# A message-passing GNN on one core: how edge records are stored and fetched again

## The reference

```python
s2 = jnp.concatenate([src, dst]); d2 = jnp.concatenate([dst, src])
ef2 = jnp.concatenate([ef, ef], axis=0)
h_prev = nf
for l in range(3):
    e_in = jnp.concatenate([h_prev[s2], h_prev[d2], ef2], axis=-1)
    msg = jax.nn.leaky_relu(e_in @ We1[l]) @ We2[l]
    red = jax.ops.segment_sum(msg, d2, num_segments=N)
    n_in = jnp.concatenate([h_prev, red], axis=-1)
    out = jax.nn.leaky_relu(n_in @ Wn1[l]) @ Wn2[l]
    h_prev = out + h_prev
# result: _layernorm(x + out)
```

## Time and profile before

| | us |
|---|---|
| median of three runs | 3773.15 (3763.34 to 3774.12) |
| the profiled execution | 3767.26 |
| its span | 3765.6 |
| PE, DVE, ACT, POOL busy | 2446.1, 2741.9, 2101.1, 776.5 |
| DMA | 564.71 MB, mean 150 GB/s |

### The profile page before, as it was taken

The page is one execution under the profiler, slowest core; times in us unless marked ns, Lnnn a source line. Parts: engine busy times, 40 slices in busy tenths (PEclk is TensorE's granted clock), DMA queues, the critical chain, the costliest instruction groups (busy, mean ns, idle before and its releaser), DMA issues.

```text
span 3765.6 us, 82355 instructions
## 1 busy us (share of the span) xinstructions
PE 2446.1 (65%) x26696; PEld 2111.7 (56%) x26697; DVE 2741.9 (73%) x3306; ACT 2101.1 (56%) x4171; POOL 776.5 (21%) x826
## 2 busy tenths in 40 slices
PE   4000000000004499999999699999999799999995
PEld 4000000000004387878787488888888588888884
DVE  8965655655622499999999677777777677777775
ACT  4000000000002377877787588888888688888884
POOL 0577777777771000000000000000000000000000
PEclk9555555555555699999999899999999899999998
DMA  8111111111004277777777355555555255555553
GB/s 245 56 31 43 44 31 43 43 31 43 17 13 133 84 251 250 255 253 250 249 258 251 122 172 186 190 188 192 187 186 173 94 190 191 186 187 189 189 191 111
DMA packets 237764, 564.71 MB, mean 150 GB/s; under 512 B 52668, under 2 KB 134530, under 8 KB 237598
## 3 DMA queue, kind: packets, MB, share of 16 engines
q1 hardware_dynamic: 210174, 548.80, 43.0%
q0 software_dynamic: 27552, 15.37, 2.1%
HBM read 413.59 MB, written 150.66 MB: 150 GB/s over the span
## 4 chain that ended last, share of the span: by engine, by line
PE 47%; DVE 11%; issue 6%; SPq 3%; DMA 2%; ACT 1%; POOL 0%; DVEq 0%; ACTq 0%; POOLq 0%
PE gath L1336 17%; PE sums L1397 13%; PE sums L1336 9%; PE gath L1329 4%; DVE loop_buf L1131 3%; DVE big L1060 3%; PE sums L1329 2%; DVE loop_buf L1148 2%; SPq L539 2%; DVE gsel L1064 2%; DMA loop_buf<-ssel_d 1%; DMA nums_d<-numb 1%; PE sums L1290 1%; PE sums L1505 1%; PE sums L1506 0%
## 5 line engine op out<-in xcount | busy, mean ns | idle before, releaser
L1060 DVE SCALAR_TENSOR_TENSOR big<-big 128x768 f32<-128x768 f32 (+1 forms) x957 | 908.4, 949 | 426.8 <-ACT big L786 387.6
L1336 PE MATMUL gath<-table,gsel 128*128 x7488 | 1075.7, 273 | 0.0
L1131 DVE TENSOR_TENSOR loop_buf<-big,loop_buf 128x768 f16<-128x768 f32 x936 | 890.4, 951 | 0.0
L650 POOL DMA_INDIRECT records<-rec,rowi x784 | 750.8, 958 | 285.6 <-issue 248.3
L1397 PE MATMUL sums<-loop_buf 128*128 128x128 f16 x11232 | 782.2, 219 | 23.8 <-issue 18.1
L1336 PEld LDWEIGHTS gath<-table,gsel 128*128 128x128 f16 x7488 | 734.1, 98 | 84.9
L790 ACT ACTIVATE loop_buf<-big 128x768 f16<-128x768 f32 x936 | 781.4, 835 | 0.0
L1397 PEld LDWEIGHTS sums<-loop_buf 128*128 128x128 f16 x11232 | 650.1, 98 | 124.5 <-ACT sums L784 58.0
L786 ACT ACTIVATE big<-gath 128x512 f32<-128x512 f32 x936 | 559.1, 597 | 278.1 <-PE gath L1336 278.1
L1252 PE MATMUL sums<-table,fchunk 128*128 128x200 f16 x196 | 37.1, 366 | 877.1 <-DVE found L976 864.7
L1336 PE MATMUL sums<-table,gsel 128*128 x3744 | 564.1, 273 | 13.2 <-DVE gsel L1064 13.2
(11 more groups left out here) (174 smaller groups left out, 1657.6 us busy)
## 6 DMA issues: line engine op xcount, KB each, us to landing
gsel<-gsel_d SPq DMA_DIRECT2D x208, 576.0 KB, 3.8
loop_buf<-ssel_d SPq DMA_DIRECT2D x208, 576.0 KB, 4.7
numb<-nums_d SPq DMA_DIRECT2D x106, 576.0 KB, 4.6
gsel_d<-gsel SPq DMA_DIRECT2D x104, 576.0 KB, 5.5
ssel_d<-loop_buf SPq DMA_DIRECT2D x104, 576.0 KB, 6.5
fchunk<-feat_d SPq DMA_DIRECT2D x1260, 40.0 KB, 1.8
loop_buf<-rows_d SPq DMA_DIRECT2D x28, 896.0 KB
records<-rec,rowi POOLq DMA_INDIRECT x784
```

What stands on the lines that cost most here:

```text
L650: pool.indirect_dma_start(out=records[:, :], out_offset=bass.IndirectOffsetOnAxis(ap=rowi[:, h, g:g + 1].bitcast(U32), axis=0), in_=rec[:, ...
L1060: return dve.scalar_tensor_tensor(m, m, SLOPE, m, ALU.mult, ALU.max)
L1131: dve.tensor_tensor(m_lo[:, place, :], msg[:, place, :], m_hi[:, place, :], ALU.subtract)\
L1336: return pe.matmul(uv, gsel[:, h, (2 * tc + s) * P:(2 * tc + s + 1) * P], at[n], start=False, stop=n == 3, skip_group_check=True)
```

## The change

Records: feat_d loses the two number rows per tile and becomes 64 rows (two tiles of 32). SP stores the features of a batch in two transfers of 32 rows each. The numbers of a batch are copied to `num16` on DVE (double-buffered), transposed on PE into 64 rows of their own, in the unused half of the bank of group h = 3, copied by DVE to `numT`, and stored in one transfer of 64 rows of 256 B. `numcol` is filled from num16. POOL's reload now waits for the num16 copy, PE waits for it ahead of h = 3, and SP for numT after it has issued the features.

Layers: a part's features come in two transfers of 64 rows instead of four of 32 (in all layers); in layers 1 and 2 they are issued behind gsel and ssel instead of ahead of them.

```diff
@@ -106,7 +106,7 @@
 def build(nc, x, src, dst, ef, We1, We2, Wn1, Wn2, c_iota, c_part, c_tri, c_ident, c_tiles, c_steps, c_below, out):
 
     records = nc.dram_tensor("records", [TILES * P, RW], F16)
-    feat_d = nc.dram_tensor("feat_d", [2, RW, (TILES // 2 + F_AHEAD * PART_PAIRS) * P], F16)
+    feat_d = nc.dram_tensor("feat_d", [4 * EF, (TILES // 2 + F_AHEAD * PART_PAIRS) * P], F16)
     nums_d = nc.dram_tensor("nums_d", [(TILES + PART) * 2, P], F16)
 
     gsel_d = nc.dram_tensor("gsel_d", [TURNS * PARTS + 1, P, PART * 2 * P], F16)
@@ -257,6 +257,8 @@
 
         recc = sb("recc", [P, SLOTS_IN, PREP, CHUNK, RW], F16)
         hrow = recc[:, :, :, :, :].rearrange("p k h t f -> p (k h t f)")[:, 0:2 * RUN * P].rearrange("p (h e) -> p h e", h=2)
+        num16 = sb("num16", [P, 2, 2 * BATCH], F16)
+        numT = sb("numT", [2 * BATCH, SLOTS_IN, P], F16)
         numcol = sb("numcol", [P, TILES * 2], F16)
         lo_b = numcol[:, 0:2 * COLS].bitcast(I32)
 
@@ -353,7 +355,8 @@
         rec_hi_seq = sem("rec_hi_seq")
         moved = [sem(f"moved{h}") for h in range(2)]
         recc_in = [sem(f"recc_in{k}") for k in range(SLOTS_IN)]
-        numcol_set = sem("numcol_set")
+        num16_set = sem("num16_set")
+        numT_set = sem("numT_set")
         tr_done = sem("tr_done")
         featA_set = sem("featA_set")
         featD_set = sem("featD_set")
@@ -416,7 +419,7 @@
         T_BLOCKS = 2 * NB // T_PARTS
         WIDE = [(n, min(BANK, NODES - n * BANK)) for n in range(BANKS)]
         YSTEPS = -(-NB // 4)
-        FEAT_DMAS = 4
+        FEAT_DMAS = 2
         EDGE_DMAS, NODE_DMAS = 2 + P // EF, 2
         
 
@@ -453,6 +456,10 @@
 
             n = k * PREP + h
             return bank(n) if n < BANKS else gath
+
+        def num_bank(k):
+
+            return tr_bank(k, PREP - 1)[0:2 * BATCH, BANK // 2:BANK // 2 + P // 2]
 
 
         block = ctx.enter_context(nc.Block())
@@ -533,18 +540,15 @@
                             sp.wait_ge(featA_set, batch * 2 + 2 + BANK_AHEAD)
                             sp.wait_ge(featD_set, batch * 2 + 2 + BANK_AHEAD)
                             sp.sem_inc(sp_go, 1)
-                            sp.dma_start(feat_d[:, :, ds(batch * (PAIR_COLS * P), PAIR_COLS * P)].rearrange("a f e -> (a f) e"),
-                                         recT[slot]).then_inc(rec_out[slot], 16)
                             for a in range(2):
-                                sp.dma_start(nums_d[ds(batch * (2 * BATCH), 2 * BATCH), :]
-                                             .rearrange("(q a s) e -> a s q e", a=2, s=2)[a],
-                                             recT[slot][a * RW + 2 * EF:(a + 1) * RW, :].rearrange("s (q e) -> s q e", e=P))\
-                                  .then_inc(rec_out[slot], 16)
+                                sp.dma_start(feat_d[a * 2 * EF:(a + 1) * 2 * EF, ds(batch * (PAIR_COLS * P), PAIR_COLS * P)],
+                                             recT[slot][a * RW:a * RW + 2 * EF, :]).then_inc(rec_out[slot], 16)
+                            sp.wait_ge(numT_set, batch + 1)
+                            sp.dma_start(nums_d[ds(batch * (2 * BATCH), 2 * BATCH), :], numT[:, slot, :]).then_inc(rec_out[slot], 16)
             for slot in range(SLOTS_IN):
                 sp.wait_ge(rec_out[slot], (live_p + (1 - slot // 2)) // 2 * (16 * OUT_DMAS) + 16 * OUT_DMAS)
 
-            sp.dma_start(feat_d[:, :, ds(live_n * (ITER_PAIRS * P), F_AHEAD * PART_PAIRS * P)].rearrange("a f e -> (a f) e"),
-                         feat_d[:, :, 0:F_AHEAD * PART_PAIRS * P].rearrange("a f e -> (a f) e")).then_inc(wrap_out, 16)
+            sp.dma_start(feat_d[:, ds(live_n * (ITER_PAIRS * P), F_AHEAD * PART_PAIRS * P)], feat_d[:, 0:F_AHEAD * PART_PAIRS * P]).then_inc(wrap_out, 16)
             sp.dma_start(nums_d[ds(live_n * (ITER * 2), 2 * PART * 2), :], nums_d[0:2 * PART * 2, :]).then_inc(wrap_out, 16)
             sp.wait_ge(wrap_out, 32)
 
@@ -556,11 +560,8 @@
 
                 pair = (turn_n + p // PARTS) * ITER_PAIRS + p % PARTS * PART // 2
                 for r in range(2):
-                    for a in range(2):
-                        at = (2 * r + a) * 2 * EF
-                        sp.dma_start(fchunk[at:at + 2 * EF, p % PARTS, :],
-                                     feat_d[a:a + 1, 0:2 * EF, ds(pair * P, PART_PAIRS * P)].rearrange("a f e -> (a f) e"))\
-                          .then_inc(fchunk_in[p % PARTS], DMA)
+                    sp.dma_start(fchunk[r * 4 * EF:(r + 1) * 4 * EF, p % PARTS, :], feat_d[:, ds(pair * P, PART_PAIRS * P)])\
+                      .then_inc(fchunk_in[p % PARTS], DMA)
 
             load_numbers(0, 0)
             load_numbers(1, 1)
@@ -589,11 +590,11 @@
                                 h, part_n = p % 2, it * PARTS + p
 
                                 sp.wait_ge(sum_done, (l * live_n + it) * STEPS + p * PART_STEPS + AHEAD)
-                                load_features(it, p + F_AHEAD)
                                 sp.dma_start(gsel[:, 1 - h, :], gsel_d[ds(part_n + 1, 1), :, :].rearrange("a p e -> (a p) e"))\
                                   .then_inc(gsel_set[1 - h], DMA)
                                 sp.dma_start(ssel_part(h), ssel_d[ds(part_n, 1), :, :].rearrange("a p e -> (a p) e"))\
                                   .then_inc(ssel_set[h], DMA)
+                                load_features(it, p + F_AHEAD)
 
                 with sp.If(l < 1):
                     for h in range(2):
@@ -663,7 +664,7 @@
                             batch = it * SLOTS_IN + k
 
                             pool.wait_ge(tr_done, (batch + 1 - SLOTS_IN) * PREP + TR_AHEAD)
-                            pool.wait_ge(numcol_set, batch + 1)
+                            pool.wait_ge(num16_set, batch + 1)
                             pool.sem_inc(pool_go, 1)
                             pool.dma_start(recc[:, k, :, :, :].rearrange("p h t f -> p h (t f)"),
                                            records[ds(batch * (BATCH * P), BATCH * P), :]
@@ -826,7 +827,7 @@
             for s in (msg_set, h_set):
                 dve.sem_inc(s, AHEAD)
             dve.sem_inc(featD_set, BANK_AHEAD)
-            dve.sem_inc(numcol_set, SLOTS_IN)
+            dve.sem_inc(num16_set, SLOTS_IN)
             dve.sem_inc(krow_free, KROW_AHEAD)
             dve.sem_inc(hrow_free, KROW_AHEAD)
             dve.sem_inc(found_set, AHEAD)
@@ -1042,11 +1043,15 @@
                             slot = half * 2 + k
                             batch = it * SLOTS_IN + slot
                             dve.wait_ge(recc_in[slot], it * 16 + 16)
-                            dve.tensor_copy(numcol[:, ds(batch * (2 * BATCH), 2 * BATCH)].rearrange("p (t s) -> p t s", s=2),
-                                            recc[:, slot, :, :, 2 * EF:RW].rearrange("p h t s -> p (h t) s")).then_inc(numcol_set, 1)
+                            dve.tensor_copy(num16[:, k, :].rearrange("p (t s) -> p t s", s=2),
+                                            recc[:, slot, :, :, 2 * EF:RW].rearrange("p h t s -> p (h t) s")).then_inc(num16_set, 1)
+                            dve.wait_ge(num16_set, batch + 1 + SLOTS_IN)
+                            dve.tensor_copy(numcol[:, ds(batch * (2 * BATCH), 2 * BATCH)], num16[:, k, :])
                             for h in range(2, PREP):
                                 dve.wait_ge(tr_done, batch * PREP + h + 1 + TR_AHEAD)
                                 dve.wait_ge(rec_out[slot], it * (16 * OUT_DMAS) + 16 * OUT_DMAS)
+                                if h == PREP - 1:
+                                    dve.tensor_copy(numT[:, slot, :], num_bank(k).bitcast(F16)).then_inc(numT_set, 1)
                                 dve.tensor_copy(recT[slot][:, h * CHUNK // 2 * P:(h + 1) * CHUNK // 2 * P],
                                                 tr_bank(k, h)[0:2 * RW, 0:CHUNK // 2 * P // 2].bitcast(F16)).then_inc(featD_set, 1)
 
@@ -1270,6 +1275,10 @@
                                 if h % 2 == 0:
                                     pe.wait_ge(featD_set if h else featA_set, batch * 2 - 2 + BANK_AHEAD)
                                     pe.sem_inc(pe_go, 1)
+                                if h == PREP - 1:
+                                    pe.wait_ge(num16_set, batch + 1 + SLOTS_IN)
+                                    pe.sem_inc(pe_go, 1)
+                                    pe.transpose(num_bank(k).bitcast(F16), num16[:, k, :], ident16[:, :])
                                 for t in range(0, CHUNK, 2):
                                     last = pe.transpose(tr_bank(k, h)[0:2 * RW, t * P // 4:(t + 2) * P // 4].bitcast(F16),
                                                         recc[:, slot, h, t:t + 2, :].rearrange("p t f -> p (t f)"), ident16[:, :])
```

## The result

| | before | after |
|---|---|---|
| median, us | 3771.98 (4 runs) | 3668.31 (4 runs) |
| ratio, 95% interval | | 0.9731 (0.9714 to 0.9748) |
| span of the profiled execution | 3765.6 | 3666.9 |

A forecast was written before the change was run, and what follows sets the result against it. The prediction took DVE to bound layer 0, PE layers 1 and 2, and slow stores the record stage. Gains of 58 + 9 + 3 = 70 us gave a median of 3703 us, ratio 0.981, range 3684 to 3738.

The forecast's parts named there:

- Bound of the record stage: Record stage: transfers don't lack total capacity; by the skill's rule 68-row stores ran on 4 engines, 4.5 us a batch estimated.
- an issue held per transfer: Record stage rival: SP is held per transfer, stores no faster, batch near 4.2 us at least, 3766 us; chance 0.04.
- 2.25 us a batch, 58 us: Record loop: a batch falls from 4.18 to 2.25 us, bounds 1.9 and 3.2; gain 58 us over 30 batches.
- PE's 2.1 us: Record loop: PE's demand per batch with one more transpose and its waits, about 2.1 us at the low clock.
- the lower of its bounds: Record loop: SP's three issues ask 1.8 us a batch, or 3.2 if the queue stays fuller.
- Tail 9 us: From the record stage's last copy to the first one-hot table: 22.9 us becomes 13.9, gain 9 us, bounds 4 and 12.
- The a/b chain: Matmuls right after the last copy, 13.6 us on PE: meets the shorter tail almost exactly, doesn't take the gain back.
- New waits: Record loop: waits for num16 and numT are hidden or cost nothing; at the double clock num16 late by some 0.1 us.
- Waits for `nums_d` of a few us in total: Record stage sign: DVE and ACT no longer wait for number stores above a few us in total.
- Fewer feature loads: All layers: two feature loads instead of four, same bytes, half the issues; worth nothing in layer 0.
- The layers' order: Layers 1 and 2: ssel issued 2.0 us earlier, ahead of features, removes PE's waits; gain 3 us, bounds 0 and 5.

The follow-up runs named there:

- ACT's issues: Changed kernel with a batch's number store issued from ACT's queue instead of SP's; median 3662.3 us, ratio to before 0.9728.

## Why the prediction was wrong

- **Bound of the record stage: right.** Uneven engines, not capacity: shown by 34, 64 and 68 rows and by the packets that overlap. The prediction could not separate this from an issue held per transfer; the store cut into 64 and 4 rows does, since it has one transfer more and is faster.
- **2.25 us a batch, 58 us: right in kind, a little high.** 2.02 us, 64.8 us. PE's 2.1 us was taken at the low clock; it was granted 2.4 GHz for most of the stage, and PE was not the limit. SP was, near the lower of its bounds (0.32, 0.31 and 0.49 us an issue): relieved of one issue, the stage took 1.92.
- **Tail 9 us: right**, 8.8 (the terms of the new tail add to 13.6 us, not to the 13.9 written; measured 14.2). The a/b chain met it as said: DVE's maxima ran on without a gap.
- **New waits: nothing, right.** PE waited 3.3 us in all for num16, SP not for numT. The numcol copy took 0.21 us and numT 0.22, where I had taken 0.18.
- **Waits for `nums_d` of a few us in total: wrong.** DVE and ACT still wait 35 us for stores of their slot (176 before, in the four groups of which the earlier trace rows have two). With SP as the slowest this is probably a wait for what SP hands over late; no run tried whether it costs anything of its own.
- **Fewer feature loads: nothing in layer 0, right** (1.5 us). In layers 1 and 2 they would have given 8.7 and 9.9 of the 11.0 and 12.9 us by themselves, had they stood ahead of ssel.
- **The layers' order: wrong, and this is the step that failed.** It read "PE waited for ssel 1.5 + 1.3 us in both layers", gain 3 us, bounds 0 and 5. Measured: 11.0 and 12.9 us. The mechanism, an earlier ssel, was right; the size was read off the waits whose releaser is named ssel. The loss stood at another instruction (the sums), under another releaser (ACT's L784, 31 times up to 0.5 us) and in part in no wait at all: PE's busy time fell from 727.7 to 721.9 us for the same matmuls when it went. What the prediction lacked is the register load of 0.85 us between the wait and the sums: a landing less than 0.67 us ahead of the third tile held the load, and the load held the sums. A comparison of the steps by their place in the loop would have shown it before the change: 2.31 us everywhere but at the last of each 24 (3.2 in both kernels), and more at the first step of some parts, 33 of 35 times in layer 1 at places 9, 15 and 21, all with a load.
- The forecast's own range, with a bound of 5 us on this term, could then not reach the result. With 24 in place of 3 the sum is 91; the 7 us more from the record stage and the 1.5 of layer 0 bring it within 1 us of the 98.7. Without this term the forecast was 67 us and the measurement 75.

## What to carry to other kernels

Count rows before a DMA store: here 68 rows in one transfer took 4.18 us a batch, the same rows as 64 and 4 took 2.56, and as 34 and 34 took 5.79. The profile showed it as waits for the transfer behind and as a held queue, at a low DMA share. To price a wait in a loop that repeats, compare the periods of its steps by place, not the waits by name, and look at what the instruction stream does between the wait and the next matmuls: a landing that comes just ahead of its use can expose work there that was hidden. What SP issues ahead of a critical load is part of that load's latency.

## What the runs showed of the hardware

- A load of registers on PE took 0.85 us (117 in layer 1, 0.845 to 0.871). Behind a wait whose semaphore rose less than 0.67 us ahead of the array's arrival it delayed the next matmuls by the missing part, in 70 of 70 cases; 36 waits with as short a lead but no load behind them cost nothing.
- That delay is named after another engine by the trace, which puts it down to the last semaphore that the delayed matmuls wait for (ACT's, risen 0.3 us before).
- A wait that stands as an instruction of its own in PE's stream, directly ahead of matmuls, cost 0.05 us each time (51 ns, 104 times a layer).
- An issue on SP took 0.25 us for the number pieces behind stores of 32 rows, and up to 4.1 us behind stores of 68 rows; one store of 64 short rows behind 68 rows took 0.49 us.
- Stores of 68, 34 and 32 or 64 rows had at most 4, 2 and 14 to 16 packets of 4 KB under way at a time, but for 2 to 4% of the time.
- The transposes' granted clock rose from 0.55 to 0.82 over the stage, and to 0.93 with ACT's issues, with no change to PE's work but one transpose a batch.
